# Router weights behind three row blocks and x on SyncE's queue, and new engine orders for the opening

## The reference, cut to what matters

```python
y = einsum('bct,bcd->bdt', x, weights[condition])      # x (64, 64, 1024), weights (16, 64, 64)
y2 = y.reshape(4096, 1024)
top1 = argmax(y2 @ gate_w.T + expert_bias)             # 4 experts
base = y @ W_up.T                                      # W_up (1024, 1024)
z = einsum('nh,erh->ner', y2, lora_A)                  # rank 8
delta = einsum('ner,ehr->neh', z, lora_B)[top1]        # of the chosen expert
return x + base + delta
```

## Time and profile before

| | us |
|---|---|
| median of 3 runs | 428.89 (428.08 to 430.2) |
| profiled execution | 428.31 |
| its span | 426.1 |
| TensorE busy | 419.4 (98%) |
| VectorE, ScalarE, GpSimd busy | 265.2, 136.3, 112.1 |

### The profile page before, as it was taken

How to read it: one execution, slowest core, us unless ns; L and a number is a source line. 1 busy time by engine, 2 the same in 40 slices (tenths; PEclk the granted TensorE clock), 3 DMA queues, 4 the chain that set the end, 5 groups by cost and what they waited for, 6 DMA issues and landing times.

```text
span 426.1 us, 8356 instructions
## 1 busy us (share of the span) xinstructions
PE 419.4 (98%) x2876; PEld 390.8 (92%) x2876; DVE 265.2 (62%) x534; ACT 136.3 (32%) x250; POOL 112.1 (26%) x91
## 2 busy tenths in 40 slices
PE   8998999999999999999999999999999999999997
PEld 8897989999999999999989998999999999999996
DVE  3999655747556484655747465574755648465583
ACT  5994223233232232323223231323323222332220
POOL 1788200405032050502305040140503105050220
PEclk9999999999999999999999999999999999999999
DMA  8810421405032050402305031140503205050202
GB/s 277 310 46 2 125 81 51 154 26 178 15 107 83 25 178 25 170 9 91 112 25 178 25 134 44 51 152 25 177 26 114 65 30 173 25 176 3 98 2 98
DMA packets 20980, 39.22 MB, mean 92 GB/s; under 512 B 7494, under 2 KB 7750, under 8 KB 20970
## 3 DMA queue, kind: packets, MB, share of 16 engines
q1 hardware_dynamic: 16736, 24.26, 16.3%
q10 hardware_dynamic: 4234, 14.83, 10.2%
HBM read 22.30 MB, written 16.78 MB: 92 GB/s over the span
## 4 chain that ended last, share of the span: by engine, by line
PE 96%; DVE 1%; DMA 1%; issue 1%; SPq 1%; ACT 0%
PE bank_y L694 22%; PE bank_x L694 21%; PE bank_c L694 20%; PE y_ps L610 12%; PE bank_b L694 10%; PE bank_x L674 1%; DMA x_sb<-in_x_dram 1%; PE bank_x L759 1%; PE bank_y L700 1%; PE bank_x L700 1%; PE bank_b L700 1%; PE bank_c L700 1%; PE bank_y L731 1%; PE y_ps L628 1%; PE bank_c L619 0%
## 5 line engine op out<-in xcount | busy, mean ns | idle before, releaser
L252 POOL TENSOR_TENSOR s_sum<-a 128x512 f32<-128x512 f32 x16 | 20.8, 1298 | 272.3 <-ACT a L410 270.1
L237 DVE TENSOR_TENSOR hl_a<-a,hl_a 128x512 fp32r<-128x512 f32 x46 | 37.2, 811 | 40.7 <-ACT hl_a L419 40.7
L410 ACT ACTIVATE a<-y_ps 128x512 f32<-128x512 f32 x56 | 33.5, 598 | 80.8 <-PE y_ps L610 80.8
L610 PE MATMUL y_ps<-cond_pair,x_sb 128*128 128x128 f32 x448 | 59.0, 275 | 0.0
L610 PEld LDWEIGHTS y_ps<-cond_pair,x_sb 128*128 128x128 f32 x448 | 54.5, 191 | 1.3
L694 PE MATMUL bank_y<-w_s,hl_s 128*128 128x292 f32 (+1 forms) x384 | 51.8, 291 | 0.0
L694 PE MATMUL bank_x<-w_a,hl_a 128*128 128x256 f32 (+1 forms) x384 | 50.9, 288 | 0.0
L694 PEld LDWEIGHTS bank_y<-w_s,hl_s 128*128 128x128 f32 x384 | 50.0, 188 | 0.6
L694 PEld LDWEIGHTS bank_x<-w_a,hl_a 128*128 128x128 f32 x384 | 49.6, 188 | 0.4
L694 PE MATMUL bank_c<-w_s,hl_s 128*128 128x512 f32 x192 | 48.6, 401 | 0.0
L694 PE MATMUL bank_b<-w_s,hl_s 128*128 128x512 f32 x192 | 48.5, 401 | 0.0
(11 more groups left out here) (152 smaller groups left out, 489.1 us busy)
## 6 DMA issues: line engine op xcount, KB each, us to landing
out_dram<-x_sb SPq DMA_DIRECT2D x63, 256.0 KB, 2.0
x_sb<-in_x_dram ACTq DMA_DIRECT2D x28, 512.0 KB, 3.4
w_raw<-in_L_ffn_W_up_dram SPq DMA_DIRECT2D x8, 512.0 KB, 5.9
x_sb<-in_x_dram SPq DMA_DIRECT2D x4, 512.0 KB, 4.7
cond_pair<-in_L_cond_weights_dram SPq DMA_DIRECT2D x64, 16.0 KB, 2.6
out_dram<-x_sb SPq DMA_DIRECT2D x2, 128.0 KB, 1.8
router_sb<-in_L_ffn_lora_A_dram ACTq DMA_DIRECT2D x1, 128.0 KB
lora_b_sb<-in_L_ffn_lora_B_dram SPq DMA_DIRECT2D x1, 128.0 KB, 6.1
```

The lines of the kernel that those rows point to most:

```text
L237: eng.tensor_tensor(hl[op][:, 1, :, :], by_k(src[:, :]), hl[op][:, 0, :, :].bitcast(fp32), ALU.subtract)\
L252: eng.tensor_tensor(s1_sum[:, :], a21[:, :], a22[:, :], ALU.add).then_inc(s1_added, 1)
L410: act.activation(to[:, :], y_ps[:, h, :], ACT.Copy).then_inc(y_summed, 1)
L610: mm = pe.matmul(y_ps[:, h, k * P:(k + 1) * P], x_sb[:, 2 * par + t, (h * KH + k) * P:(h * KH + k + 1) * P], cond_pair[:, 2 * par + t, :], ...
```

## The change

Three parts. The two loads of router_sb go from ScalarE's queue, where they were the second and third issue, to SyncE's, between W_up rows 2 and 6. The bank tables are new, and the order in which the halves of y are made. The hand-written orders of the opening on TensorE, ScalarE, VectorE and GpSimd are new; each has the same calls with the same sizes as before, but `low_sum(2, 2)` and `low_sum(1, 1)` go from VectorE to GpSimd and `low_sum(2, 3)` from GpSimd to VectorE. The diff without the four order lists:

```diff
--- before.py
+++ after.py
@@ -198,15 +198,15 @@
         TURNED, HIGH, LOW = 1, 2, 3
         FORMED = 1
         WEIGHT_OF = {"b11": "a11", "b21": "a12", "b22": "s4", 1: "s1", 2: "s2", 3: "s3", 4: "a22"}
-        BANK_OF = {("b21", 0): (bank_b, 0), ("b11", 0): (bank_y, 0), ("b12", 0): (y_ps, 1),
-                   ("b22", 0): (bank_x, 0), "gate": (bank_y, 1), ("b11", 1): (y_ps, 1),
-                   ("b21", 1): (bank_x, 1), ("b12", 1): (bank_y, 1), ("b22", 1): (bank_x, 0),
-                   ("b11", 2): (bank_y, 1), ("b12", 2): (y_ps, 0), ("b22", 2): (bank_c, 0),
-                   ("b11", 3): (y_ps, 0), ("b12", 3): (y_ps, 1), ("b22", 3): (y_ps, 1), "lora0": (bank_c, 0),
-                   "lora1": (bank_b, 0), ("b21", 2): (y_ps, 1), ("b21", 3): (y_ps, 0)}
-        LAST_TURNED = ("b21", 3)
-        FIRST_Y = [(0, 1), (0, 0), (1, 0), (1, 1), (2, 0), (3, 0), (3, 1), (2, 1)]
-        FIRST_Y_BANK = [(y_ps, 0), (y_ps, 0), (bank_x, 0), (y_ps, 0), (bank_c, 0), (bank_b, 0), (bank_c, 0), (bank_b, 0)]
+        BANK_OF = {("b21", 0): (bank_c, 0), ("b11", 0): (bank_x, 1), ("b12", 0): (bank_y, 0),
+                   ("b22", 0): (bank_b, 0), ("b11", 1): (bank_x, 0), ("b21", 1): (bank_y, 0),
+                   ("b12", 1): (bank_b, 0), ("b22", 1): (y_ps, 1), ("b21", 2): (bank_y, 1),
+                   "gate": (bank_b, 0), ("b11", 2): (bank_x, 1), ("b22", 2): (bank_c, 0),
+                   ("b12", 2): (y_ps, 0), ("b12", 3): (y_ps, 0), ("b21", 3): (bank_b, 0),
+                   ("b11", 3): (y_ps, 1), ("b22", 3): (y_ps, 0), "lora0": (bank_b, 0), "lora1": (y_ps, 0)}
+        LAST_TURNED = ("b22", 3)
+        FIRST_Y = [(0, 0), (0, 1), (1, 1), (1, 0), (2, 0), (2, 1), (3, 0), (3, 1)]
+        FIRST_Y_BANK = [(bank_y, 1), (y_ps, 0), (y_ps, 1), (y_ps, 0), (bank_c, 0), (y_ps, 0), (y_ps, 1), (y_ps, 0)]
         Y_AT = {name: n + 1 for n, name in enumerate(FIRST_Y)}
 
         def bank_of(name):
@@ -297,6 +297,8 @@
             sp.dma_start(x_sb[:, 0, :], x_pairs[0]).then_inc(x_loaded[0], 16)
             load_w_up(5)
             load_w_up(2)
+            sp.dma_start(router_sb[0:E, :], gate_w).then_inc(router_loaded, 16)
+            sp.dma_start(router_sb[E:GC, :], lora_a.rearrange("e r t -> (e r) t")).then_inc(router_loaded, 16)
             load_w_up(6)
             load_first_pair(0, 1)
             sp.dma_start(x_sb[:, 1, :], x_pairs[1]).then_inc(x_loaded[1], 16)
@@ -394,8 +397,6 @@
         @block.scalar
         def _(act):
             act.dma_start(index_sb[:, :], cond_index.rearrange("(a n) -> a n", a=1)).then_inc(index_loaded, 16)
-            act.dma_start(router_sb[0:E, :], gate_w).then_inc(router_loaded, 16)
-            act.dma_start(router_sb[E:GC, :], lora_a.rearrange("e r t -> (e r) t")).then_inc(router_loaded, 16)
             act.wait_ge(bias_zero, 1)
             act.dma_start(bias_sb[:, 0:E], expert_bias.rearrange("(a n) -> a n", a=1).to_broadcast([P, E]))\
                 .then_inc(bias_loaded, 16)
```

More of the change, by code:

```diff
@@ L765, in _ @@
             turn("b11", 0)
-            warm_up(2, bank_x[:, 1, :])
+            warm_up(2, bank_y[:, 1, :])
             turn("b12", 0)
             turn("b22", 0)
-            turn_gate()
-            wait_piece_read("b12", 0)
-            turn("b11", 1)
-            turn("b21", 1)
-            make_first_y(0, 1)
-            pe.wait_ge(gate_stage, LOW)
-            turn("b12", 1)
-            wait_piece_read("b22", 0)
-            turn("b22", 1)
-            wait_y_moved(0, 1)
-            make_first_y(0, 0)
-            wait_piece_read("b12", 1)
-            turn("b11", 2)
-            wait_y_moved(0, 0)
-            turn("b12", 2)
-            turn("b22", 2)
-            wait_piece_read("b22", 1)
-            make_first_y(1, 0)
-            wait_piece_read("b12", 2)
-            make_first_y(1, 1)
-            wait_piece_read("b11", 0)
+            turn("b11", 1)
+            wait_piece_read("b12", 0)
+            turn("b21", 1)
+            make_first_y(0, 0)
+            wait_piece_read("b22", 0)
+            turn("b12", 1)
+            turn("b22", 1)
+            make_first_y(0, 1)
+            wait_y_moved(0, 0)
+            turn("b21", 2)
+            wait_piece_read("b12", 1)
+            turn_gate()
+            wait_piece_read("b11", 0)
+            turn("b11", 2)
+            wait_piece_read("b21", 0)
+            turn("b22", 2)
+            wait_y_moved(0, 1)
+            turn("b12", 2)
+            wait_piece_read("b22", 1)
+            make_first_y(1, 1)
+            wait_piece_read("b12", 2)
+            make_first_y(1, 0)
+            wait_piece_read("b11", 1)
+            wait_pieces("b11", 0)
+            pe.wait_ge(gate_stage, LOW)
+            multiply_half("a11", 0, bank_x, True)
+            wait_y_moved(1, 0)
+            turn("b12", 3)
+            pe.wait_ge(gate_stage, LOW)
+            turn("b21", 3)
+            wait_y_moved(1, 1)
+            turn("b11", 3)
+            wait_piece_read("b12", 3)
+            turn("b22", 3)
+            wait_piece_read("b21", 1)
             wait_pieces("b21", 0)
@@ L818, in _ @@
             multiply_half("s2", 0, bank_x, False)
-            wait_piece_read("b11", 3)
-            turn("b21", 3)
-            wait_y_moved(2, 0)
-            make_first_y(3, 1)
+            wait_piece_read("b21", 2)
+            wait_pieces("b21", 1)
+            multiply_half("a12", 1, bank_y, True)
             wait_sums(2, 1)
             multiply_half("s2", 1, bank_x, False)
-            wait_piece_read("b11", 2)
-            wait_pieces("b21", 1)
-            multiply_half("a12", 1, bank_y, True)
+            wait_piece_read("b11", 3)
+            make_first_y(3, 0)
+            wait_piece_read("b21", 3)
+            turn_lora(0)
             wait_sums(3, 0)
@@ L1087, in _ @@
             low_sum(dve, 1, 3)
-            low_operand(dve, "a11", a11, 1)
-            low_sum(dve, 4, 3)
-            low_sum(dve, 1, 1)
             after_p7(0, 0)
```

191 lines of the change are left out of this document (90 added, 101 removed).

## The result

The changed kernel takes 431.50 us (430.35 to 431.94, 10 runs), the kernel before beside it 429.17 (428.06 to 430.20, 10 runs): ratio 1.0058, 95% interval 1.0041 to 1.0074. By the ratio it is 2.5 us slower, where 428.0 was forecast, and its median lies outside the range. Of all the executions told of here two ran far slower (517 and 2362 us) and are in no ratio or median.

What follows compares the result with a forecast made beforehand. TensorE, busy 98%, was the bound, with 3.91 us idle in the opening. Gains of 1.8 us by s1's end (0.07 by x of pair 1), less 0.95 for route 2, leave 0.9: 428.89 becomes 428.0 us, range 426.1 to 430.3.

Steps and rivals of the forecast that it cites:

- So I keep 9.98 us: Opening: x of pair 0 lands at 9.98 us as before, at most 0.38 us earlier.
- x of pair 1 ... 15.74: Opening: x of pair 1 lands at 15.74 us in place of 15.36, so y(1,1) starts at 15.97.
- 0.38 us later: Full queue from 7.6 to 15 us: the router's 147 KB at 382 GB/s delay x of pair 1 by 0.38 us.
- about 1 us is free there: SyncE's queue between W_up rows 2 and 6: free time hides the router's two issues, 0.3 us each.
- Route 1, "0.3 us idle": Before the first transposition of z: routing takes about 4 us beside GpSimd; TensorE idles 0.3 us in place of 0.96.
- the forecast's bound of 4.6 for a fourth wait: First route on VectorE: upper bound of its length, 4.6 us, if a fourth step waits for GpSimd.
- Route 2, 43.95, "the new wait ... 0.95": Second transposition of z: routing steps wait for GpSimd, TensorE turns z at 43.95 us, taking 0.95 us back.
- 22.30 us: TensorE from y(1,1) through s3's second half: 22.30 us of work, ending at 38.27 if nothing waits.
- thin covers that hold: Bank readers and operands between y(1,1) and first z: ready 0.15 to 0.6 us before needed, so no cost taken.
- router there at 13.0: Gate transposition: router lands at 13.0 us, 0.65 us before the gate at 13.65 wants it.
- rival 4: Router comes late: past 14.0 us each us costs one; landing at 15 us gives 429.0; chance 0.04.
- Rival 3, the clock: TensorE's clock falls in the 1.25 us idle from 8.8: 1.2 us slower, 430.1 us; chance 0.06.

Runs made afterwards that it cites:

- e9: The kernel before, unchanged, profiled once more: this execution took 431.04 us.
- e5: Changed kernel plus eight warm-up matmuls on TensorE between b21,1 and y(0,0), where it waits for x of pair 0: ratio to before 1.0030.
- e6: Changed kernel plus two waits that hold GpSimd back until the first and the second route are done: ratio to before 0.9991, median 428.7 us.
- e10: Changed kernel with the router loads back on ScalarE's queue at the start and two waits holding GpSimd back during the routes: ratio to before 0.9968.
- e1: Changed kernel with the router loads back on ScalarE's queue, new orders kept: ratio to before 1.0026, median 430.89 us.
- e13: As e10, but the router loads are issued later on ScalarE's queue, after b11,0 is rounded (5.4 and 5.7 us): ratio to before 1.0015.
- e14: As e10, but the router loads are issued early on SyncE's queue, right behind W_up row 1: ratio to before 0.9979.
- e2: Kernel before with only the router loads moved to SyncE's queue between W_up rows 2 and 6, old orders and banks: ratio to before 1.0155.
- e8: Changed kernel with x of pair 0 issued ahead of its two small weight loads: ratio to before 1.0022, median 430.73 us.
- e11: Kernel before plus one wait: GpSimd holds back low s4 and the two sums behind it until the first route is done: ratio to before 0.9997.

## Why the prediction was wrong, point by point

- *"So I keep 9.98 us"* and *"x of pair 1 ... 15.74"*: the steps that failed first. They took the landings of one execution as the kernel's. e9 shows 11.8 for x of pair 0 and a start of pair 1 at 18.42 in the same kernel; in 14 traces of all versions x of pair 0 is issued behind its small loads, and only in the forecast's did it land before 10.7 us. In the changed kernel's trace x of pair 1 landed at 17.9, 2.1 us past the forecast: 0.6 by a later issue (11.48 against 10.88), 1.5 by a longer way (6.4 us against 4.5 and the 0.38 added). The half clock between 11.0 and 14.3 put TensorE back as far (7.2 us from y(0,0) to y(1,1) against 5.9 in the forecast), so that both were there at 18.0; with the clock held, y(1,1) still started at 18.08 (e5). Since both kernels have such executions, this explains the level of the trace, and not by itself the ratio.
- *"0.38 us later"* for the router's bytes: mis-sized. x of pair 1 needs about 1.0 us more from issue to landing over all traces, and the time is 1.0 us longer by e6 and e10, 1.4 by the changed kernel and e1 (0.6 by their medians), 2.0 by e13 and e10. The term took the 382 GB/s of one trace for the stretch with the router in it, which ran at 290 to 306. That it is the time and not the queue was tested by e13 and e14. It is what the Trainium skill leads one to expect ("DMA: Bandwidth & Descriptors", "Issuing engines are not separate DMA queues": transfers from all engines share 16 DMA engines), and within the intervals the runs agree. Why 147 KB weigh so much is only argued: they lie on 36 of 128 partitions, and they landed 2.5 us later than the sum of bytes says (e2).
- *"about 1 us is free there"* for the router's issues: did not hold in the changed kernel's trace, where row 6 could have gone up to 0.8 us sooner without them. It made no difference that can be told: x of pair 1 was issued at 10.8 to 11.5 us in the seven traces with the router's issues there, and at 10.3 to 11.5 in the six with them at the start of ScalarE's queue.
- *Route 1, "0.3 us idle"*: mis-sized, 1.39. The mechanism was right, but four steps met a GpSimd instruction, not three, and each lost 0.8 to 1.0 us. The route took 5.4 us (36.34 to 41.73), beyond the forecast's bound of 4.6 for a fourth wait.
- *Route 2, 43.95, "the new wait ... 0.95"*: right in size and cause, 1.02 us, with two steps waiting. The Trainium skill ("SBUF — State Buffer", the shared port pair) has the rule that of two instructions that need that pair the later one waits for the whole of the other. e6 bears it out: wherever GpSimd is silent no step waits.
- *"22.30 us"* for the walk between, and thin covers that hold: right (18.17 to 40.5).
- *"router there at 13.0"*: wrong, about 15.5 in e2, 14.6 in e8. It cost nothing in the changed kernel because x of pair 0 was later still. With x at the forecast's 9.98 the gate would have been wanted at 13.65, and so awaited for 1 to 2 us (an estimate from these landings): rival 4 would have come true.
- *Rival 3, the clock*: its event came, 0.50 for 3.3 us, with a mean clock of 0.996 in 7 of 10 executions. But it comes in 57 of 118 of the kernel before too, and x of pair 1 hides most of it. It is not what made the changed kernel slower.

Together, by the ratios: the orders 1.1 us slower (e1) where 0.9 faster was forecast, with 2.4 us of waits before the two transpositions of z in place of 0.96, and the router's place 1.4 more, which makes 2.5. The direction is sure; the sizes are not, to some 0.5 to 1 us, since the last term is only the difference of two ratios.

## What to carry to other kernels

A landing read from one execution is one draw. Where an opening hangs on transfers in a full queue, look at the spread of the runs, and profile again, before a margin of a few tenths is built on it. The same holds for a median of ten executions of a kernel whose executions spread over 2 us. A chain of small dependent VectorE steps is a bad neighbour for GpSimd's long instructions: two added waits that keep GpSimd silent during the routes gave 2.3 to 2.9 us here, where 0.9 had been forecast from all the new orders. In the kernel before, one such wait gave nothing that can be told (e11), so look first at what the engines then wait for. Small loads belong where the queue has room, before it fills.
